# A landing buffer for the moved blocks of a feed-forward unit, and the split taken from it

## The chip, the cores and the metric

The kernel runs on one core of one Trainium2 chip. The metric is the device time of one execution in microseconds (us), the median of several runs. A core has a matrix engine (TensorE, PE in the rows; PEld are its weight loads), a vector engine (VectorE, DVE), a scalar engine (ScalarE, ACT), GpSimd (POOL) and a sync engine (SyncE, SP), whose queue issues the DMA transfers. Each engine works through its own instructions in order and waits on semaphores for the others.

## What is computed

The input x holds 8 sequences of 1024 tokens with 256 features, 8192 tokens in all. Four residual layers follow one another:

```
x = x + attention(layernorm(x))            # 2 heads, causal softmax
x = x + ffn(layernorm(x))
x = x + linear_attention(layernorm(x))     # 8 heads with decay
x = x + ffn(layernorm(x))                  # the same weights again

def ffn(x):                                # w_*: integers times 1/127
    gate = x @ wg.T;  up = x @ wu.T        # 256 -> 768
    return (silu(gate) * up) @ wd.T        # 768 -> 256
```

All is float32. For its matmuls the kernel writes an activation as a high part in the type float32r and a low part, x minus the high part, also float32r, and multiplies both.

## The kernel before

The kernel runs four phases in turn (attention_phase, feed_forward_phase as ff1, linear_attention_phase, feed_forward_phase as ff2), and x stays in on-chip memory as X all the while. Within a phase the order of every engine's work is written out by hand, one function per engine, with semaphores between them.

A feed-forward phase works in 16 **units** of 512 tokens (UN), counted u = 0 to 15. The buffers of neighbouring units alternate by a parity, par. run_units (L854) writes units 0, 13, 14 and 15 out and runs 1 to 12 in a hardware loop, two per pass. left says what comes after a unit: 2 means that two more units of the phase follow, 1 that one does, 0 that none does. In a unit the 768 hidden features are worked through in six **slots**, f = 0 to 5, of 128 features each (NF = 6). What the engines do in a slot:

- TensorE (L1044 to L1060) computes gate(f), then up(f) (L1026), four matmuls each, and then down(f-3) (L1037), the last projection of the slot three earlier (LAG = 3), eight matmuls. Slots 3, 4 and 5 of a unit are thus projected down in slots 0, 1 and 2 of the next. Gate and up have three banks each (NB_GU = 3), so gate(f) waits for the silu of slot f-3, up(f) for the h of slot f-3, and down waits for the high and the low part of its h. Ahead of its first slot a unit waits for its high and low parts (front.pe_wait, L1045).
- ScalarE (L943 to L954) takes silu(f) (L951) and then the high part of h of slot f-1 (L941).
- VectorE (L984 to L1004) takes h(f) = silu(f) * up(f) (L990), which waits for silu(f), then the low part of h of slot f-1 (L974). In slot 2 comes the residual of the unit before (L981).

Between these stands the preparation of later units, and it is what the change touches. It runs over these steps:

- In unit u VectorE prepares unit u+2: statistics of the layernorm in slots 0 and 1 (L132, L140), normalise in slot 3, behind h(3) and the low part of slot 2 (L156, four instructions), and in slot 4, behind h(4) and the low part of slot 3, one transpose of 32x32 blocks (dve_blocks, L255) from one half of ln_xn into the other. Here "blocks of unit u+2" names that result. The transpose waits for the move of unit u+1 to have landed, for that move reads the same buffer.
- GpSimd computes the reciprocal deviation for the normalise (L167, L170).
- In unit u SyncE moves the blocks of unit u+1 across partitions with 16 DMAs of 32 KB (sp_move, L266), which finishes the transpose. Their target is the low half of the pair of unit u+1, ln_xl or ff_odd_xl by parity. First it waits until the last up projection of unit u-1, which reads that pair, has ended (L893), then for the blocks of unit u+1.
- In slot 4 of unit u ScalarE waits for that landing, and takes the high part of unit u+1 from it (act_high, L271). In its order this stands ahead of silu(4).
- GpSimd then subtracts the high part from what landed, in place (pool_low, L276), which finishes the pair of unit u+1.

In unit 15 of ff1 the same steps prepare the first unit of the linear attention; in ff2 nothing follows, and SyncE also stores the finished tokens of unit u-1 behind the move (L904).

The order by hand in ScalarE's function is this:

```
for f in range(NF):
    if f == NF - 2 and upcoming:
        nfront.act_high(act, nu, npar)      # waits for the landing
    ...silu(f)...
    high_part(u, par, f - 1)
```

Of the kernel before, what the change touches and what calls it, by code (L numbers as in the profile page):

```python
# [13 lines left out]
F32 = mybir.dt.float32  # L14
# [4 lines left out]
ACT = mybir.ActivationFunctionType  # L19
AX = mybir.AxisListType  # L20

P = 128
NB, T, M = 8, 1024, 256
KT = M // P
# [3 lines left out]
UN = UT * P  # L28
# [14 lines left out]
NF = FF // P  # L43
# [16 lines left out]
class Signal:  # L60


    def __init__(self, nc, ctx, name, per):
        self.sem = ctx.enter_context(nc.semaphore(name))
        self.per = per
# [6 lines left out]
def open_signals(eng, *signals):  # L72

    for s in signals:
        eng.sem_inc(s.sem, CREDIT)


def wait_alone(eng, sem, value, passed):


    eng.wait_ge(sem, value)
    eng.sem_inc(passed, 1)
# [140 lines left out]
class Turned:  # L223
# [4 lines left out]
    def __init__(self, nc, ctx, name, ln, blocks, parts, unit=0):  # L228
        sig = lambda n, per: Signal(nc, ctx, f"{name}_{n}", per)
        self.nc, self.ln, self.blocks, self.unit = nc, ln, blocks, unit  # L230
        self.parts = [parts, parts]
        self.blocks_done = sig("blocks_done", 1)
        self.landed = sig("landed", 16 * MOVES)
        self.sp_passed = ctx.enter_context(nc.semaphore(f"{name}_sp_passed"))
        self.hi_done, self.lo_done = sig("hi_done", 1), sig("lo_done", 1)
# [19 lines left out]
        self.nc.vector.transpose(self.blocks.rearrange("p t m -> p (t m)"),  # L255
                                 self.ln.out[:, self.unit * UT:(self.unit + 1) * UT, :].rearrange("p t m -> p (t m)")).then_inc(self.blocks_done.sem, 1)

    def sp_move(self, sp, unit, par):

        wait_alone(sp, self.blocks_done.sem, self.blocks_done.at(unit, 1), self.sp_passed)  # L260
        lo = self.parts[par][1][:].bitcast(F32)
        for r in range(NQ):
            for c in range(NQ):
                src = self.blocks[r * SQ:(r + 1) * SQ, c, :].rearrange("p (n b) -> p n b", b=SQ)
                dst = lo[c * SQ:(c + 1) * SQ].rearrange("p k (t r b) -> p (k t) r b", t=UT, r=NQ)[:, :, r, :]
                sp.dma_start(dst, src).then_inc(self.landed.sem, 16)  # L266

    def act_high(self, act, unit, par):
        hi, lo = self.parts[par]
        act.wait_ge(self.landed.sem, self.landed.at(unit, 16 * MOVES))  # L270
        self.nc.scalar.activation(hi[:], lo[:].bitcast(F32), ACT.Copy).then_inc(self.hi_done.sem, 1)  # L271

    def pool_low(self, pool, unit, par):
        hi, lo = self.parts[par]
        pool.wait_ge(self.hi_done.sem, self.hi_done.at(unit, 1))  # L275
        self.nc.gpsimd.tensor_tensor(lo[:], lo[:].bitcast(F32), hi[:].bitcast(F32),  # L276
                                     ALU.subtract).then_inc(self.lo_done.sem, 1)

    def pe_wait(self, pe, unit):
# [529 lines left out]
def load_lin_weights(eng, env, io):  # L809
    stage = env["stage"]  # L810
    eng.dma_start(stage[:, 0:KT * LB_COLS].rearrange("p (k n) -> p k n", k=KT),
                  io["w_lin"].rearrange("(k p) n -> p k n", p=P)).then_inc(env["lin_loaded"], 16)
    eng.dma_start(stage[:, KT * LB_COLS:KT * LB_COLS + NP * M].rearrange("p (k m) -> p k m", k=NP),
                  io["w_o"].rearrange("(k p) m -> p k m", p=P)).then_inc(env["lin_loaded"], 16)


def feed_forward_phase(nc, env, io, name, nth, front, following):
# [5 lines left out]
    with ExitStack() as ctx:  # L823
        sb = lambda n, shape, dt=F32: ctx.enter_context(nc.sbuf_tensor(f"{name}_{n}", shape, dt))
# [9 lines left out]
        down_hi, down_lo = (w[:, parts_of_w[2]].rearrange("p (k m) -> p k m", k=NF) for w in (w_hi, w_lo))  # L834
        ln = front.ln
        front.parts[1] = sb("odd_xh", [P, KT, UN], F32R), sb("odd_xl", [P, KT, UN], F32R)
        sx = [front.pair(0), front.pair(1)]
        NB_GU = 3
        silu = sb("silu", [P, NB_GU, UN])
# [6 lines left out]
        gate_ready, up_ready = sig("gate_ready", NF), sig("up_ready", NF)  # L846
# [7 lines left out]
        def run_units(eng, unit):  # L854


            unit(0, 0, True, 2)
            with eng.Fori(0, NU // 2 - 2) as p:
                unit(p * 2 + 1, 1, False, 2)
                unit(p * 2 + 2, 0, False, 2)  # L860
            unit(NU - 3, 1, False, 2)
            unit(NU - 2, 0, False, 1)
            unit(NU - 1, 1, False, 0)

        def slot(par, f):

            return (NF * par + f) % NH

        def next_of(u, par, left):

            if left:
                return front, u + 1, 1 - par
            return (following, 0, 0) if following else None

        def after_next(u, left):

            if left == 2:
                return front, u + 2
            return (following, 0) if left and following else None

        with nc.Block() as block:

            @block.sync
            def _(sp):
                if following:
                    following.sp_open(sp)

                def unit(u, par, first, left):
                    upcoming = next_of(u, par, left)
                    if upcoming:  # L890
                        nfront, nu, npar = upcoming
                        if not first:
                            wait_alone(sp, up_ready.sem, up_ready.at(u - 1, NF), front.sp_passed)  # L893
                        nfront.sp_move(sp, nu, npar)
                    if following and first:
                        sp.wait_ge(prep_lo, NPART)
                        load_lin_weights(sp, env, io)
                    if not following and not first:
                        store(u - 1)

                def store(u):
                    wait_alone(sp, x_done.sem, x_done.at(u, 1), front.sp_passed)
                    at = bass.ds(u * UT, UT)
                    sp.dma_start(out_v[:, at, :], X[:, at, :]).then_inc(stored, 16)  # L904

                run_units(sp, unit)
                if not following:
                    store(NU - 1)
                    sp.wait_ge(stored, 16 * NU)

            @block.gpsimd
            def _(pool):
                if following:
                    following.pool_open(pool)

                def unit(u, par, first, left):
                    upcoming, after = next_of(u, par, left), after_next(u, left)
                    if after:
                        after[0].ln.pool_rstd(pool, after[1])
                    if upcoming:  # L920
                        nfront, nu, npar = upcoming
                        nfront.pool_low(pool, nu, npar)

                run_units(pool, unit)

            @block.scalar
            def _(act):
                if following:
                    following.act_open(act)
                open_signals(act, silu_done, hi_done)  # L930
                for at in parts_of_w:
                    if split_before:
                        nc.scalar.activation(w_lo[:, at], stage[:, at], ACT.Copy).then_inc(prep_lo, 1)
                    else:
                        act.wait_ge(env["ff_loaded"], 16 * NPART * nth)
                        nc.scalar.activation(w_hi[:, at], stage[:, at].bitcast(I32), ACT.Copy).then_inc(prep_hi, 1)  # L936

                def high_part(u, par, f):
                    act.wait_ge(h_done.sem, h_done.at(u, f + 1))
                    act.wait_ge(down_done.sem, down_done.at(u, f - NH + 1))  # L940
                    nc.scalar.activation(h_hi[:, slot(par, f), :], h[:, f % 2, :], ACT.Copy).then_inc(hi_done.sem, 1)  # L941

                def unit(u, par, first, left):  # L943
                    upcoming = next_of(u, par, left)
                    for f in range(NF):
                        if f == NF - 2 and upcoming:
                            nfront, nu, npar = upcoming
                            nfront.act_high(act, nu, npar)
                        act.wait_ge(gate_ready.sem, gate_ready.at(u, f + 1))
                        act.wait_ge(h_done.sem, h_done.at(u, f - NB_GU + 1))  # L950
                        nc.scalar.activation(silu[:, f % NB_GU, :], PS[:, f % NB_GU, :], ACT.Silu,  # L951
                                             scale=W_SCALE).then_inc(silu_done.sem, 1)
                        if f > 0 or not first:
                            high_part(u, par, f - 1)  # L954
                    if not left:
                        high_part(u, par, NF - 1)

                run_units(act, unit)

            @block.vector  # L960
# [678 lines left out]
```

## Time and profile before

| what | value |
|---|---|
| median of 3 runs | 1981.17 us (1980.4 to 1982.3) |
| the profiled execution, its own time | 1982.85 us |
| its span, first to last instruction | 1981.1 us |
| mean granted TensorE clock | 0.994 of full speed |
| busy share: PE, PEld, DVE, ACT, POOL | 95%, 83%, 69%, 45%, 23% |
| ff1, first matmul to last | about 565 to 846 us |
| ff2, first matmul to last | about 1698 to 1976 us |

The shares are averages over the four phases, and matmuls are pipelined, so a PE that is busy 95% of the time is not at its peak. A row of the chronological view gives the start, the duration, the engine, the line, the operation, what it writes and reads, and in brackets the idle time of the engine just before it with what ended it. SPq is the queue of SyncE; of a row with x16 the duration runs from the first issue to the end of the last.

### The profile page before, as it was taken

Reading aid. Unit: us, or ns where it says so; the run is one execution under the profiler, and the core shown is the slowest. Engines: PE = TensorE matmul, PEld = TensorE weight load, DVE = VectorE, ACT = ScalarE, POOL = GpSimd, SP = SyncE. Lnnn points to the kernel's source line nnn. Section 1 sums busy time; section 2 is a strip of 40 time slices with the busy share of each in tenths; the row PEclk is TensorE's granted clock in tenths of the full one; section 3 lists DMA queues with packets and bytes.
Section 4 is the critical chain, followed back from the end, with each engine's and each line's share of the span. In section 5 each row is a group of like instructions: output and inputs, shape, how many; then the busy total and the mean of one; then the engine's idle time right before and its main releaser. Section 6 shows DMA issues by size and latency. Waiting matters only on the chain. (4 is left out here: it accounts for less than half of the span.)

```text
span 1981.1 us, 36996 instructions
## 1 busy us (share of the span) xinstructions
PE 1891.3 (95%) x12419; PEld 1639.4 (83%) x12419; DVE 1367.3 (69%) x3222; ACT 889.7 (45%) x1708; POOL 451.7 (23%) x362
## 2 busy tenths in 40 slices
PE   6999999999989999969999999999999998899998
PEld 5888888888778888858888888888888887788887
DVE  6666566656667888756766667766666677778885
ACT  5555556655654444453333333333333332444443
POOL 2112201220312222132222222222222222221220
PEclk9999999999999999989999999999999999999999
DMA  6100000000021111110000000000000000122222
GB/s 217 58 1 0 0 0 0 0 0 0 12 75 30 30 30 30 32 53 11 12 12 12 11 11 11 11 11 11 11 11 11 11 12 12 32 64 63 53 61 58
DMA packets 230887, 53.23 MB, mean 27 GB/s; under 512 B 209952, under 2 KB 229024, under 8 KB 230432
## 3 DMA queue, kind: packets, MB, share of 16 engines
q1 hardware_dynamic: 229696, 49.54, 11.7%
q10 hardware_dynamic: 1120, 2.75, 0.4%
q8 instruction: 43, 0.70, 0.2%
q14 instruction: 28, 0.23, 0.0%
HBM read 18.69 MB, written 8.39 MB: 14 GB/s over the span
## 5 line engine op out<-in xcount | busy, mean ns | idle before, releaser
L990 DVE SCALAR_TENSOR_TENSOR ff_h<-PS,ff_silu 128x512 f32<-128x512 f32 x192 | 130.9, 682 | 121.9 <-PE PS L1026 53.2
L951 ACT ACTIVATE ff_silu<-PS 128x512 f32<-128x512 f32 x192 | 114.0, 595 | 199.7 <-PE PS L1026 199.7
L1214 POOL TENSOR_TENSOR lin_yg_lo<-stage,lin_yg_hi 128x512 fp32r<-128x512 f32 x64 | 82.0, 1281 | 504.5 <-ACT lin_yg_hi L1248 504.5
L1037 PE MATMUL PS<-ff_w_hi,ff_h_hi 128*128 128x256 f32 x768 | 191.3, 282 | 2.1 <-ACT ff_h_hi L941 1.4
L1037 PE MATMUL PS<-ff_w_hi,ff_h_lo 128*128 128x256 f32 x768 | 191.9, 283 | 0.0
L318 PE MATMUL PS<-ln_xh,lin_w_hi 128*128 128x512 f32 x384 | 153.4, 400 | 15.6 <-DVE lin_w_lo L1293 8.6
L974 DVE TENSOR_TENSOR ff_h_lo<-ff_h,ff_h_hi 128x512 fp32r<-128x512 f32 x192 | 164.2, 855 | 0.2
L1026 PE MATMUL PS<-ln_xh,ff_w_hi 128*128 128x512 f32 x384 | 152.0, 396 | 11.6 <-issue 4.5
L730 PE MATMUL PS<-probT,v_a 128*128 128x128 f32 x1152 | 154.0, 279 | 4.3 <-DVE oT_lo L589 4.3
L1324 DVE TENSOR_TENSOR lin_AD<-PS,lin_decay 128x512 f32<-128x512 f32 x128 | 82.2, 684 | 109.9 <-PE PS L1470 109.9
L1037 PEld LDWEIGHTS PS<-ff_w_hi,ff_h_hi 128*128 128x128 f32 x768 | 145.6, 190 | 13.7 <-issue 2.9
L1026 PE MATMUL PS<-ff_odd_xh,ff_w_hi 128*128 128x512 f32 x384 | 151.8, 395 | 5.2 <-issue 2.4
L730 PEld LDWEIGHTS PS<-probT,v_a 128*128 128x128 f32 x1152 | 138.9, 192 | 19.5 <-issue 12.9
L318 PE MATMUL PS<-ln_xh,lin_w_lo 128*128 128x512 f32 x384 | 151.3, 394 | 0.0
L1037 PEld LDWEIGHTS PS<-ff_w_hi,ff_h_lo 128*128 128x128 f32 x768 | 146.3, 190 | 6.0
L318 PE MATMUL PS<-ln_xl,lin_w_hi 128*128 128x512 f32 x384 | 151.0, 393 | 0.0
L1026 PE MATMUL PS<-ff_odd_xl,ff_w_hi 128*128 128x512 f32 x384 | 150.8, 393 | 0.0
L1026 PE MATMUL PS<-ln_xl,ff_w_hi 128*128 128x512 f32 x384 | 150.6, 392 | 0.0
L702 PE MATMUL PS<-qk 128*128 128x512 f32 (+3 forms) x384 | 144.7, 488 | 0.0
L594 DVE TENSOR_REDUCE neg_max<-PS 128x1 f32<-128x256 f32 (+7 forms) x128 | 96.6, 755 | 65.5 <-PE PS L705 64.3
L455 POOL TENSOR_TENSOR qk<-qk,swapped 64x512 f32<-64x512 f32 x64 | 81.9, 1280 | 256.1 <-DVE swapped L584 254.2
L271 ACT ACTIVATE ln_xh<-ln_xl 128x1024 fp32r<-128x1024 f32 x32 | 33.9, 1060 | 232.2 <-DMA ln_xl<-ln_xn 232.2
(159 smaller groups left out, 4893.1 us busy)
## 6 DMA issues: line engine op xcount, KB each, us to landing
ln_xl<-ln_xn SPq DMA_DIRECT2D x512, 32.0 KB, 2.0
X<-in_x SPq DMA_DIRECT2D x8, 1024.0 KB, 5.3
ff_odd_xl<-ln_xn SPq DMA_DIRECT2D x256, 32.0 KB, 2.0
out_x<-X SPq DMA_DIRECT2D x16, 512.0 KB, 2.9
stage<-in_w_lin SPq DMA_DIRECT2D x1, 2048.0 KB, 8.2
stage<-in_w_gate SPq DMA_DIRECT2D x2, 768.0 KB, 4.3
stage<-in_w_up SPq DMA_DIRECT2D x2, 768.0 KB, 5.8
stage<-in_w_down SPq DMA_DIRECT2D x2, 768.0 KB, 7.5
```

The costliest lines, as they stand in the source:

```text
L318: last = nc.tensor.matmul(out, w, x, start=n == 0, stop=n == len(terms) - 1)
L455: done = nc.gpsimd.tensor_tensor(qk[rows, s, h, at], qk[rows, s, h, at], swapped[rows, 2 * half + s, :], ALU.add)
L594: nc.vector.tensor_reduce(neg_max[:, n:n + 1], score_rows(n), AX.X, ALU.max, negate=True).then_inc(max_done.sem, 1)
L702: last = nc.tensor.matmul(bank[:, 0:w], qk[:, 0, h, i * P:(i + 1) * P], qk[:, 1, h, c:c + w], start=True, stop=not diag)
L730: last = nc.tensor.matmul(O, V[:, j, h * DA:(h + 1) * DA], probT[:, n % 2, j, :], start=j == 0, stop=j == i)
L951: nc.scalar.activation(silu[:, f % NB_GU, :], PS[:, f % NB_GU, :], ACT.Silu, scale=W_SCALE).then_inc(silu_done.sem, 1)
L974: nc.vector.tensor_tensor(h_lo[:, slot(par, f), :], h[:, f % 2, :], h_hi[:, slot(par, f), :].bitcast(F32), ALU.subtract).then_inc(lo_done. ...
L990: nc.vector.scalar_tensor_tensor(h[:, f % 2, :], PS[:, NB_GU + f % NB_GU, :], W_SCALE, silu[:, f % NB_GU, :], ALU.mult, ALU.mult).then_inc ...
L1026: ins = nc.tensor.matmul(PS[:, bank, :], w, x, start=n == 0, stop=n == len(parts) - 1)
L1037: ins = nc.tensor.matmul(Y[:, t // 2, (t % 2) * M:(t % 2 + 1) * M], a[:, slot(par, f), t * P:(t + 1) * P], w[:, f % NF, :], start=f == 0 a ...
L1214: nc.gpsimd.tensor_tensor(yg_lo[:], yg, yg_hi[:].bitcast(F32), ALU.subtract).then_inc(yg_lo_done.sem, 1)
L1324: nc.vector.tensor_tensor(AD[:, c % 2, r], PS[:, r, :].rearrange("p (j t) -> p j t", t=P), D[:].rearrange("p (j r) t -> p r j t", r=2)[:, ...
```

## The change

A buffer raw of the size of one half of a pair (128 x 1024 float32) is added to each feed-forward phase. The move of a unit's blocks lands in it whenever the unit belongs to the same phase (raw=bool(left)); ScalarE takes the high part from raw, and GpSimd subtracts the high part from raw and writes the low half of the pair. Three things in the order change with it. SyncE waits ahead of the move of unit u+1 for the low part of unit u (the last reader of raw), and not for the last up projection of unit u-1. ScalarE waits for that projection in SyncE's place. And ScalarE takes the high part of the coming unit in slot 3 (NF - 3), ahead of silu(3), and no longer in slot 4. The move into the linear attention's first unit keeps the old target, wait and slot.

```diff
--- before.py
+++ after.py
@@ -229,6 +229,7 @@
         sig = lambda n, per: Signal(nc, ctx, f"{name}_{n}", per)
         self.nc, self.ln, self.blocks, self.unit = nc, ln, blocks, unit
         self.parts = [parts, parts]
+        self.raw = None
         self.blocks_done = sig("blocks_done", 1)
         self.landed = sig("landed", 16 * MOVES)
         self.sp_passed = ctx.enter_context(nc.semaphore(f"{name}_sp_passed"))
@@ -255,25 +256,29 @@
         self.nc.vector.transpose(self.blocks.rearrange("p t m -> p (t m)"),
                                  self.ln.out[:, self.unit * UT:(self.unit + 1) * UT, :].rearrange("p t m -> p (t m)")).then_inc(self.blocks_done.sem, 1)
 
-    def sp_move(self, sp, unit, par):
+    def landing(self, par, raw):
+
+        return self.raw[:] if raw else self.parts[par][1][:].bitcast(F32)
+
+    def sp_move(self, sp, unit, par, raw=False):
 
         wait_alone(sp, self.blocks_done.sem, self.blocks_done.at(unit, 1), self.sp_passed)
-        lo = self.parts[par][1][:].bitcast(F32)
+        lo = self.landing(par, raw)
         for r in range(NQ):
             for c in range(NQ):
                 src = self.blocks[r * SQ:(r + 1) * SQ, c, :].rearrange("p (n b) -> p n b", b=SQ)
                 dst = lo[c * SQ:(c + 1) * SQ].rearrange("p k (t r b) -> p (k t) r b", t=UT, r=NQ)[:, :, r, :]
                 sp.dma_start(dst, src).then_inc(self.landed.sem, 16)
 
-    def act_high(self, act, unit, par):
+    def act_high(self, act, unit, par, raw=False):
         hi, lo = self.parts[par]
         act.wait_ge(self.landed.sem, self.landed.at(unit, 16 * MOVES))
-        self.nc.scalar.activation(hi[:], lo[:].bitcast(F32), ACT.Copy).then_inc(self.hi_done.sem, 1)
-
-    def pool_low(self, pool, unit, par):
+        self.nc.scalar.activation(hi[:], self.landing(par, raw), ACT.Copy).then_inc(self.hi_done.sem, 1)
+
+    def pool_low(self, pool, unit, par, raw=False):
         hi, lo = self.parts[par]
         pool.wait_ge(self.hi_done.sem, self.hi_done.at(unit, 1))
-        self.nc.gpsimd.tensor_tensor(lo[:], lo[:].bitcast(F32), hi[:].bitcast(F32),
+        self.nc.gpsimd.tensor_tensor(lo[:], self.landing(par, raw), hi[:].bitcast(F32),
                                      ALU.subtract).then_inc(self.lo_done.sem, 1)
 
     def pe_wait(self, pe, unit):
@@ -834,6 +839,7 @@
         down_hi, down_lo = (w[:, parts_of_w[2]].rearrange("p (k m) -> p k m", k=NF) for w in (w_hi, w_lo))
         ln = front.ln
         front.parts[1] = sb("odd_xh", [P, KT, UN], F32R), sb("odd_xl", [P, KT, UN], F32R)
+        front.raw = sb("raw", [P, KT, UN])
         sx = [front.pair(0), front.pair(1)]
         NB_GU = 3
         silu = sb("silu", [P, NB_GU, UN])
@@ -889,9 +895,12 @@
                     upcoming = next_of(u, par, left)
                     if upcoming:
                         nfront, nu, npar = upcoming
-                        if not first:
+                        if left:
+                            if not first:
+                                wait_alone(sp, front.lo_done.sem, front.lo_done.at(u, 1), front.sp_passed)
+                        else:
                             wait_alone(sp, up_ready.sem, up_ready.at(u - 1, NF), front.sp_passed)
-                        nfront.sp_move(sp, nu, npar)
+                        nfront.sp_move(sp, nu, npar, raw=bool(left))
                     if following and first:
                         sp.wait_ge(prep_lo, NPART)
                         load_lin_weights(sp, env, io)
@@ -919,7 +928,7 @@
                         after[0].ln.pool_rstd(pool, after[1])
                     if upcoming:
                         nfront, nu, npar = upcoming
-                        nfront.pool_low(pool, nu, npar)
+                        nfront.pool_low(pool, nu, npar, raw=bool(left))
 
                 run_units(pool, unit)
 
@@ -943,9 +952,11 @@
                 def unit(u, par, first, left):
                     upcoming = next_of(u, par, left)
                     for f in range(NF):
-                        if f == NF - 2 and upcoming:
+                        if f == (NF - 3 if left else NF - 2) and upcoming:
                             nfront, nu, npar = upcoming
-                            nfront.act_high(act, nu, npar)
+                            if left and not first:
+                                act.wait_ge(up_ready.sem, up_ready.at(u - 1, NF))
+                            nfront.act_high(act, nu, npar, raw=bool(left))
                         act.wait_ge(gate_ready.sem, gate_ready.at(u, f + 1))
                         act.wait_ge(h_done.sem, h_done.at(u, f - NB_GU + 1))
                         nc.scalar.activation(silu[:, f % NB_GU, :], PS[:, f % NB_GU, :], ACT.Silu,
```

## Rows read from the trace of the kernel before

**Rows 1.** The page, busy time and share of the span of each engine:
```profile
PE 1891.3 (95%) x12419; PEld 1639.4 (83%) x12419; DVE 1367.3 (69%) x3222; ACT 889.7 (45%) x1708; POOL 451.7 (23%) x362
```

**Rows 2.** Waits of SyncE's queue, 600 to 800 us: total, times, longest:
```profile
SPq L82 <- PE PS L1026: 41.1, 11, 4.0
SPq L82 <- DVE ln_xn L255: 31.9, 12, 4.3
```

**Rows 3.** Chronological view of SyncE's queue, one move of ff1:
```profile
721.25 10.46 SPq L266 DMA_DIRECT2D ln_xl<-ln_xn  x16
```

**Rows 4.** The same view, ScalarE, slot 4 of three units in a row:
```profile
698.78 1.06 ACT L271 ACTIVATE ln_xh<-ln_xl 128x1024 fp32r<-128x1024 f32 x1 [2.71 <-DMA ln_xl<-ln_xn]
...
715.90 1.06 ACT L271 ACTIVATE ff_odd_xh<-ff_odd_xl 128x1024 fp32r<-128x1024 f32 x1 [2.61 <-DMA ff_odd_xl<-ln_xn]
716.87 0.58 ACT L951 ACTIVATE ff_silu<-PS 128x512 f32<-128x512 f32 x1
...
733.09 1.06 ACT L271 ACTIVATE ln_xh<-ln_xl 128x1024 fp32r<-128x1024 f32 x1 [2.66 <-DMA ln_xl<-ln_xn]
```

**Rows 5.** The same view, VectorE, slots 3 and 4 of that unit:
```profile
713.70 0.68 DVE L974 TENSOR_TENSOR ff_h_lo<-ff_h,ff_h_hi 128x512 fp32r<-128x512 f32 x1
714.30 1.38 DVE L156 TENSOR_SCALAR ln_xn<-X,ln_mean_var,ln_rstd 128x256 f32 x4
717.54 0.69 DVE L990 SCALAR_TENSOR_TENSOR ff_h<-PS,ff_silu 128x512 f32<-128x512 f32 x1 [1.85 <-issue]
718.14 1.86 DVE L974 TENSOR_TENSOR ff_h_lo<-ff_h,ff_h_hi 128x512 fp32r<-128x512 f32 x1
719.92 1.23 DVE L255 STREAM_TRANSPOSE ln_xn<-ln_xn 128x1024 f32<-128x1024 f32 x1
```

**Rows 6.** The same view, GpSimd, the low part of the coming unit:
```profile
717.04 2.41 POOL L276 TENSOR_TENSOR ff_odd_xl<-ff_odd_xl,ff_odd_xh 128x1024 fp32r<-128x1024 f32 x1 [6.18 <-ACT ff_odd_xh L271]
```

**Rows 7.** The same view, TensorE, from one unit into the next:
```profile
701.97 0.28 PE L1037 MATMUL PS<-ff_w_hi,ff_h_hi 128*128 128x256 f32 x1
702.09 0.28 PE L1037 MATMUL PS<-ff_w_hi,ff_h_lo 128*128 128x256 f32 x1
702.57 0.49 PE L1026 MATMUL PS<-ln_xh,ff_w_hi 128*128 128x512 f32 x1 [0.20 <-POOL ln_xl L276]
```

**Rows 8.** The page, groups: a GpSimd subtraction out of one buffer into another:
```profile
L1214 POOL TENSOR_TENSOR lin_yg_lo<-stage,lin_yg_hi 128x512 fp32r<-128x512 f32 x64 | 82.0, 1281 | 504.5 <-ACT lin_yg_hi L1248 504.5
```

**Rows 9.** The first unit of ff1, VectorE and ScalarE:
```profile
575.29 1.06 ACT L271 ACTIVATE ff_odd_xh<-ff_odd_xl 128x1024 fp32r<-128x1024 f32 x1 [0.71 <-DMA ff_odd_xl<-ln_xn]
...
575.85 3.47 DVE L156 TENSOR_SCALAR ln_xn<-X,ln_mean_var,ln_rstd 128x256 f32<-128x256 f32 x4
579.24 0.68 DVE L990 SCALAR_TENSOR_TENSOR ff_h<-PS,ff_silu 128x512 f32<-128x512 f32 x1
...
580.44 1.23 DVE L255 STREAM_TRANSPOSE ln_xn<-ln_xn 128x1024 f32<-128x1024 f32 x1
```

**Rows 10.** The first unit of ff2, ScalarE and VectorE:
```profile
1707.99 1.06 ACT L271 ACTIVATE ff_odd_xh<-ff_odd_xl 128x1024 fp32r<-128x1024 f32 x1 [0.44 <-DMA ff_odd_xl<-ln_xn]
...
1713.45 1.23 DVE L255 STREAM_TRANSPOSE ln_xn<-ln_xn 128x1024 f32<-128x1024 f32 x1
```

**Rows 11.** High parts taken last in ff1 and in ff2:
```profile
837.73 1.06 ACT L271 ACTIVATE ln_xh<-ln_xl 128x1024 fp32r<-128x1024 f32 x1 [2.75 <-DMA ln_xl<-ln_xn]
...
1952.83 1.06 ACT L271 ACTIVATE ff_odd_xh<-ff_odd_xl 128x1024 fp32r<-128x1024 f32 x1 [3.65 <-DMA ff_odd_xl<-ln_xn]
```

**Rows 12.** Two idle times of TensorE, late in linear attention and into ff2:
```profile
1680.73 1.24 PE L1499 MATMUL PS<-lin_v,lin_ks 128*128 128x130 f32 x4 [3.15 <-DVE lin_ks L1319]
...
1698.05 0.47 PE L1026 MATMUL PS<-ln_xh,ff_w_hi 128*128 128x512 f32 x1 [2.64 <-ACT ff_w_hi L936]
```

**Rows 13.** Stretches around them: length, busy times by engine, granted clock, DMA:
```profile
1676.00:1682.00 6.00, 2.85 (x21) 2.66 (x19) 5.31 (x11) 0.63 (x1) 1.36 (x1) 0.79 0.00 0
1682.00:1688.00 6.00, 6.00 (x36) 5.97 (x35) 3.90 (x13) 0.13 (x1) 0.00 (x0) 0.64 0.01 3
...
1697.00:1702.00 5.00, 3.85 (x16) 2.92 (x17) 4.17 (x3) 4.97 (x5) 0.00 (x0) 1.00 0.29 46
```

## The prediction

> **What bounds the kernel now.** The page's first part shows TensorE busy for 95% of the span [rows 1], which invites the reading that only matmul time counts. It is an average, and a matmul row is longer than the pitch at which matmuls follow one another, so I read one feed-forward unit in order of time, engine by engine, looking for the chain that closes from unit to unit.
>
> The natural start is the waits of SyncE's queue, since the change replaces one of them. Over 200 us, nearly 12 units, it waited 41.1 us for TensorE's up projection and 31.9 us for the transposed blocks [rows 2]. A reader may take the first number for the price of the wait that is removed. But the two waits stand one behind the other ahead of each move, and the blocks come last: in one unit the transpose starts at 719.92 and takes 1.23, so it ends at 721.15 [rows 5], and the first DMA is issued at 721.25 [rows 3]. The wait for TensorE had by then been over for some time. What starts a move is the transpose.
>
> From there the chain runs on. All times are starts unless said otherwise:
> - first DMA 721.25, high part 733.09 [rows 3, 4]: 11.84 us, of which 10.46 is issuing the 16 DMAs one after another. ScalarE had idled 2.66 us for this landing.
> - high part 715.90, silu(4) behind it 716.87 [rows 4], h(4) 717.54, low part of slot 3 718.14, transpose 719.92 [rows 5]: 4.02 us from high part to transpose. The low part took 1.86 us where the same operation took 0.68 at 713.70 [rows 5]; GpSimd's own subtraction ran from 717.04 to 719.45 [rows 6], and VectorE's low part ended 0.55 us after it. I read this as VectorE held back until GpSimd was done.
> - transpose 719.92 to first DMA 721.25: 1.33 us.
>
> The sum is 4.02 + 1.33 + 11.84 = 17.19 us from one high part to the next, and rows 4 show just that from 715.90 to 733.09, and 17.16 on average over two units from 698.78. TensorE is not in this chain. It fills its unit and then waits 0.36 us: the down matmuls start 0.12 apart, the last at 702.09, so the next could start at 702.21, and it came at 702.57 [rows 7]. So TensorE alone needs 17.12 (698.78 to 715.90) - 0.36, about 16.8 us per unit. **The feed-forward phases are bound by the chain landing, high part, silu, h, low part, transpose, move, landing, with TensorE close below it.**
>
> One more thing matters in the same rows: VectorE does its normalise (714.30, 1.38 us) while it would otherwise idle; even so it idled 1.85 us before h(4) [rows 5]. Today that work costs the chain nothing.
>
> **The change part by part.** *SyncE's wait.* Removed: the wait for the up projection, worth nothing, since the transpose ends later. Added: a wait for the low part of unit u. It ends 719.45 in rows 6, ahead of the transpose's end at 721.15, so it costs nothing either: SyncE gets no earlier start from the new buffer. In ff2 the store stands behind the move in the same queue, and waits for a residual of slot 2; nothing there is new.
>
> *ScalarE's wait for the up projection.* In steady state it has long been met when the landing comes, for ScalarE idles 2.6 us there [rows 4]. Cost nothing; cover is that idle time.
>
> *The buffer.* The high part and the subtraction read as many elements as before, from another address. I take 1.06 and 2.41 us as they are [rows 4, 6]. No row shows this subtraction from one buffer into another. The nearest one of half the size does, 1.28 us [rows 8]; twice that, 2.56, counts its fixed part twice and is the upper bound, 0.15 us more in each link, some 4 us in all. Below, the bound is no change, since the elements and types are the same; rows 6 are the same operation, so I take them.
>
> *The high part in slot 3.* This is the part that costs. It can't be taken before its blocks land, and they land about 12 us behind the transpose in slot 4 of the unit before. ScalarE works in order, so silu(3) is now held by the landing, where it was silu(4). Behind silu(3) VectorE's order is h(3), low part of slot 2, normalise, h(4), low part of slot 3, transpose. So from the high part on:
> - silu(3) takes the place of silu(4), h(3) that of h(4), the low part of slot 2 that of slot 3, still held by GpSimd: the next VectorE instruction starts 4.02 us after the high part, as the transpose did.
> - it is the normalise, whose cover is gone: 1.38 us, and the next start comes 0.08 before a row's end (575.85 + 3.47 against 579.24 in rows 9), so 1.30.
> - h(4) and the low part of slot 3: 0.60 each from start to start (717.54 to 718.14, and 713.70 to 714.30 for a low part that isn't held, in rows 5). GpSimd is idle by then.
> - transpose at 4.02 + 1.30 + 0.60 + 0.60 = 6.52 us.
>
> The link becomes 6.52 + 1.33 + 11.84 = 19.69 us, **2.50 us more in every unit**. TensorE needs 16.8, so it no longer sets anything, and idles 2.9 us per unit, in slot 5 ahead of down(2), which waits for the held low part.
>
> Could the phase settle elsewhere, with the landing ahead of slot 3? A unit paced by TensorE alone has slots of 2.8 us. up(4) would end 4 x 2.8 + 1.9 = 13.1 us into the unit; h(4), a low part and the transpose follow at 0.6 + 0.6 + 1.2, the move adds 11.8 and the hand-over 0.1: landed 27.4 us after the unit's start, 10.6 into the next. gate(3) is ready at 3 x 2.8 + 0.9 = 9.3. So even from an undisturbed start silu(3) is late, and the chain above takes over.
>
> *How many links.* ff1 prepares units 1 to 15 and then the linear attention's first unit, which makes 15 links between 16 high parts (575.29 to 837.73 [rows 9, 11]); 14 of them gain 2.50 = 35.0. In the first, the normalise is caught by GpSimd already (3.47 us) and the transpose came at 575.29 + 5.15; it moves to + 6.52, a cost of 1.4. The last high part stays in slot 4, and the end of ff1 hangs on it as before. ff1: 36.4 us. ff2 has 14 links; 13 x 2.50 = 32.5, and the first costs 1707.99 + 6.52 - 1713.45 = 1.1 [rows 10]. Behind its last high part (1952.83 [rows 11]) the last unit starts once down(2) is through, 4.1 + 0.9 = 5.0 us later, where it started 702.57 - 698.78 = 3.8 after the high part in steady state [rows 4, 7], so 1.2 more. ff2: 34.8 us. Attention and linear attention keep their instructions.
>
> **Sum:** 36.4 + 34.8 = 71.2 us on the profiled execution's 1982.85 us: 2054.1. That execution stands 1.7 us above the median of the runs, so for the median I say 1981.2 + 71.2 = **2052.4 us**, 3.6% slower.
>
> *The clock.* TensorE's granted clock is at the full level of 2.4 GHz in the feed-forward phases. One idle time of 3.15 us at 1680.73 [rows 12] was followed by a fall: 0.79 and 0.64 granted in two stretches of 6 us, between its two levels, 1.2 and 2.4 GHz [rows 13]. One of 2.64 us at 1698.05 was not: 1.00 [rows 12, 13]. The new idle time, 2.9 us, lies between. If it fell each time as it did there, the loss would be 6 x 0.21 + 6 x 0.36 = 3.4 us of matmul work, against 2.9 us of slack: 0.5 us per unit over some 29 units, 14 us more. I leave it out of the sum, since the slack takes nearly all and a unit without slack has no idle time to cause the next fall.
>
> The Trainium skill, page "TensorE: Matmul & The Clock Gate", section "Why this matters for your kernels", speaks against this change here: it warns that idle stretches between bursts of matmuls bring the lower clock back. By it the sum would be the clock case's 2066; rows 12 and 13 agree for one idle time and not for the other.
>
> **The rivals.**
> - *The buffer lets the moves start early (faster).* For it: 41.1 us of waiting for TensorE [rows 2]. If that wait were the last, the chain would fall below TensorE's pace and each phase would run at 16.8 per unit: ff1 837.73 - 575.29 - 15 x 16.76 = 11.0, ff2 1952.83 - 1707.99 - 14 x 16.76 = 10.2 [rows 9 to 11], so about 1960. It decides once the landing comes before gate(3) is ready. Against it: the move starts 0.1 us behind the transpose. 4%.
> - *The place of the high part makes no difference (the same).* For it: silu results have three buffers and the down projections lag by three slots, so late silus need not stop TensorE. Against it: it is VectorE's transpose, not TensorE, that is delayed. About 1981. 3%.
> - *VectorE gets ahead of GpSimd.* If the low part of slot 2 weren't held (0.68 instead of 1.86), a link would gain 1.2 less: 2.50 - 1.18 = 1.3, or 71 - 28 x 1.18 = 38: 2019. Against it: GpSimd starts 1.1 us behind the high part, 1.1 us ahead of the low part, as now. 3%.
> - *The clock falls as well:* 2066, or somewhat above if the lower level lasts longer. 9%.
> - The chain as worked out, 2052: 81%.
>
> **How the numbers follow.** 0.2% (4 us) is about what measurement can tell from no change. Faster 0.04, same 0.03, slower 0.93. Within the main case the link's cost may lie between 2.2 and 2.8 us (hand-overs, and a stretch of DMA issues that takes 11.3 in place of 10.4), 9 us either way. With the clock case the range is 2041 to 2067; it leaves out the low rivals.
>
> **What would show it.** Right: in slot 3 ScalarE idles for the DMA before the high part, 19.7 us from one high part to the next; the normalise directly behind a low part of 1.8 us; the transpose 6.5 us behind the high part; the first DMA 0.1 us behind the transpose's end; TensorE idle some 2.9 us per unit at L1037, waiting for the low part of h; the linear attention as long as before. Wrong: a move issued before the transpose ends (impossible by its data), high parts 17 us apart or closer, or a granted clock well below 1 in ff1.

## The result, and the profile after

| | before | after |
|---|---|---|
| median | 1981.74 us (4 runs) | 2054.07 us (4 runs, 2053.64 to 2057.85) |
| span of the profiled execution | 1981.1 us | 2051.8 us |
| mean granted clock | 0.994 | 0.981 |

The change makes the kernel slower: ratio 1.037, 95% interval 1.0352 to 1.0388. Forecast were 2052.4 us and a range of 2041 to 2067.

The page of the changed kernel, its busy times and one group of its fifth part (TensorE's down projection), against [rows 1]:

```profile
PE 1913.5 (93%) x12419; PEld 1653.6 (81%) x12419; DVE 1361.4 (66%) x3222; ACT 887.6 (43%) x1708; POOL 458.2 (22%) x362
...
L1048 PE MATMUL PS<-ff_w_hi,ff_h_hi 128*128 128x256 f32 x768 | 201.1, 293 | 60.7 <-DVE ff_h_lo L985 59.0
```

The instructions of the computing engines are the same in number, and none got more than a little busier (TensorE's 22 us more go with its lower clock, on which more below). What is new is 59 us in which TensorE waits at the down projection for a low part of h. (Lines have moved: act_high is L276, pool_low L281, transpose L256, h L1001, its low part L985, down L1048, the move's DMA L271.)

The chronological view of the changed kernel, ScalarE, which answers to [rows 4]:

```profile
716.20 1.06 ACT L276 ACTIVATE ln_xh<-ff_raw 128x1024 fp32r<-128x1024 f32 x1 [5.03 <-DMA ff_raw<-ln_xn]
717.16 0.58 ACT L962 ACTIVATE ff_silu<-PS 128x512 f32<-128x512 f32 x1
...
735.81 1.06 ACT L276 ACTIVATE ff_odd_xh<-ff_raw 128x1024 fp32r<-128x1024 f32 x1 [6.51 <-DMA ff_raw<-ln_xn]
```

VectorE between the two, which answers to [rows 5], and GpSimd, to [rows 6]:

```profile
717.83 0.69 DVE L1001 SCALAR_TENSOR_TENSOR ff_h<-PS,ff_silu 128x512 f32<-128x512 f32 x1 [4.44 <-ACT ff_silu L962]
718.44 1.84 DVE L985 TENSOR_TENSOR ff_h_lo<-ff_h,ff_h_hi 128x512 fp32r<-128x512 f32 x1
720.21 1.37 DVE L156 TENSOR_SCALAR ln_xn<-X,ln_mean_var,ln_rstd 128x256 f32 x4
721.50 0.69 DVE L1001 SCALAR_TENSOR_TENSOR ff_h<-PS,ff_silu 128x512 f32<-128x512 f32 x1
722.10 0.68 DVE L985 TENSOR_TENSOR ff_h_lo<-ff_h,ff_h_hi 128x512 fp32r<-128x512 f32 x1
722.70 1.24 DVE L256 STREAM_TRANSPOSE ln_xn<-ln_xn 128x1024 f32<-128x1024 f32 x1
...
717.34 2.40 POOL L281 TENSOR_TENSOR ln_xl<-ff_raw,ln_xh 128x1024 fp32r<-128x1024 f32 x1 [6.03 <-ACT ln_xh L276]
```

And the queue of SyncE, to [rows 3], in a window from 715 to 728 us, which cuts the row off after 7 of the 16 DMAs:

```profile
724.03 4.51 SPq L271 DMA_DIRECT2D ff_raw<-ln_xn  x7
```

Read them in the order of the chain. The landing releases the high part at 716.20. Behind it come silu(3), h(3), the held low part of slot 2, the normalise, h(4), the low part of slot 3 and, 6.50 us after the high part, the transpose. The first DMA is issued 1.33 later, and the next high part is taken at 735.81: 19.61 us in all, where it was 17.2. Before, VectorE did the normalise and then idled 1.85 us for silu(4); now it idles 4.44 us for silu(3), and all that stands in slot 3 comes behind.

### The profile page after: what moved, and what is told of

It is laid out like the page before. It is cut to its first block and busy times, and to the rows that moved or that the text cites. A ratio compares the mean times of both kernels' runs of the same rounds, so it can differ in the third digit from the quotient of the medians.

```text
span 2051.8 us, 37000 instructions
## 1 busy us (share of the span) xinstructions
PE 1913.5 (93%) x12419; PEld 1653.6 (81%) x12419; DVE 1361.4 (66%) x3222; ACT 887.6 (43%) x1708; POOL 458.2 (22%) x362
## 5 line engine op out<-in xcount | busy, mean ns | idle before, releaser
L1001 DVE SCALAR_TENSOR_TENSOR ff_h<-PS,ff_silu 128x512 f32<-128x512 f32 x192 | 130.3, 679 | 196.8 <-ACT ff_silu L962 118.4
L1048 PE MATMUL PS<-ff_w_hi,ff_h_hi 128*128 128x256 f32 x768 | 201.1, 293 | 60.7 <-DVE ff_h_lo L985 59.0
L1048 PEld LDWEIGHTS PS<-ff_w_hi,ff_h_hi 128*128 128x128 f32 x768 | 151.3, 197 | 83.7 <-issue 73.2
L1048 PE MATMUL PS<-ff_w_hi,ff_h_lo 128*128 128x256 f32 x768 | 198.2, 289 | 0.0
L323 PE MATMUL PS<-ln_xh,lin_w_hi 128*128 128x512 f32 x384 | 152.5, 397 | 16.7 <-DVE lin_w_lo L1304 16.3
L985 DVE TENSOR_TENSOR ff_h_lo<-ff_h,ff_h_hi 128x512 fp32r<-128x512 f32 x192 | 165.8, 863 | 0.2
L950 ACT ACTIVATE ff_h_hi<-ff_h 128x512 fp32r<-128x512 f32 x192 | 120.3, 627 | 97.7 <-DVE ff_h L1001 97.5
L1048 PEld LDWEIGHTS PS<-ff_w_hi,ff_h_lo 128*128 128x128 f32 x768 | 151.9, 198 | 5.2
L1037 PE MATMUL PS<-ff_odd_xl,ff_w_hi 128*128 128x512 f32 x384 | 156.1, 406 | 0.0
```

The costliest lines, as they stand in the source:

```text
L323: last = nc.tensor.matmul(out, w, x, start=n == 0, stop=n == len(terms) - 1)
L985: nc.vector.tensor_tensor(h_lo[:, slot(par, f), :], h[:, f % 2, :], h_hi[:, slot(par, f), :].bitcast(F32), ALU.subtract).then_inc(lo_done. ...
L1001: nc.vector.scalar_tensor_tensor(h[:, f % 2, :], PS[:, NB_GU + f % NB_GU, :], W_SCALE, silu[:, f % NB_GU, :], ALU.mult, ALU.mult).then_inc ...
L1037: ins = nc.tensor.matmul(PS[:, bank, :], w, x, start=n == 0, stop=n == len(parts) - 1)
L1048: ins = nc.tensor.matmul(Y[:, t // 2, (t % 2) * M:(t % 2 + 1) * M], a[:, slot(par, f), t * P:(t + 1) * P], w[:, f % NF, :], start=f == 0 a ...
```

## The experiments

Six kernels ask what the cost consists of, four what is to be had by the same reading. Those told as a single run have no interval. "Link" is the time from one high part to the next in the middle of ff1.

| label | what it is | us | link |
|---|---|---|---|
| before | | 1981 | 17.2 |
| changed kernel | | 2054 | 19.6 |
| e1_raw_slot4 | buffer and waits, high part in slot 4 | 1982.1 | 17.2 |
| e2_before_slot3 | no buffer, high part in slot 3 | 2053.9 | 19.6 |
| e3_norm_first | normalise ahead of h(3) | 2021.6 | 18.6 |
| e7_turn_slot4_head | transpose at the head of slot 4 | 2026.0 | 18.7 |
| e8_half_low | half of GpSimd's subtraction | 2022.1 | 18.5 |
| e4_slot2 | high part in slot 2 | 2191.0 | 23.9 to 25.1 |
| e5_before_turn_first | before, transpose ahead of h(4) | 1964.2 | 16.8 |
| e6_after_turn_first | changed, both at the head of slot 3 | 1977.1 | 17.2 |
| e9_norm_slot2 | as e6, normalise in slot 2 | 2095.6 | 20.2 to 22.9 |
| e10_turn_first_slot4 | as e6, high part in slot 4 | 1966.8 | 16.8 |

**The two halves of the change apart (e1, e2).** e1, against the changed kernel:

```diff
-                        if f == (NF - 3 if left else NF - 2) and upcoming:
+                        if f == NF - 2 and upcoming:
```

> The changed kernel with the high part of the coming unit back in slot 4; the buffer raw and both new waits stay. By the chain (the cost is VectorE's normalise, h(4) and low part put between landing and transpose) everything comes back: 17.2 us from one high part to the next, 1982 us, give or take 3. If the cost comes from the buffer or from SyncE's wait for the low part, it stays near 2054. If it were the late silus holding TensorE, slot 4 would give back only the part of one slot, with a figure between the two.

e2 makes the same edit the other way round in the kernel before, and nothing else.

> The kernel before with the high part in slot 3 and nothing else: no buffer, old waits. By the chain it costs all that the change costs: 19.6 us per unit, 2053 us, give or take 4. If the buffer or its waits cost something, it comes out lower by that; if they are the whole cost, 1982.

e1: 1982.11 us, ratio to before 0.9999, interval 0.9987 to 1.0011. e2: 2053.93, ratio 1.0357 (1.0337 to 1.0377). e2 in the chronological view, ScalarE and VectorE:

```profile
714.05 1.06 ACT L271 ACTIVATE ln_xh<-ln_xl 128x1024 fp32r<-128x1024 f32 x1 [5.02 <-DMA ln_xl<-ln_xn]
...
733.65 1.06 ACT L271 ACTIVATE ff_odd_xh<-ff_odd_xl 128x1024 fp32r<-128x1024 f32 x1 [6.52 <-DMA ff_odd_xl<-ln_xn]
...
720.54 1.23 DVE L255 STREAM_TRANSPOSE ln_xn<-ln_xn 128x1024 f32<-128x1024 f32 x1
```

The transpose comes 6.49 us behind the high part and the link is 19.60, without any buffer. So the whole cost is the slot of the high part, and the buffer with its two waits is worth nothing that e1 can tell, which is some 2 us either way. That is so although SyncE's row of waits grew. The waits of its queue over the whole changed kernel:

```profile
SPq L82 <- POOL ln_xl L281: 63.3, 14, 5.0
SPq L82 <- POOL ff_odd_xl L281: 57.4, 14, 4.8
```

These 120.7 us stand where 95.0 us of waiting for TensorE stood. Neither is a price, for behind them in the same queue stands the wait for the blocks, which ends last: in the rows of the changed kernel GpSimd's low part was done at 719.74 and the transpose at 723.94, and the first DMA came at 724.03.

**The terms of the link, one at a time (e3, e7, e8, e4).** e3 and e7 move an operation of VectorE out of the chain:

```diff
 e3: for f in range(NF):
+    if after and f == 3: after[0].ln.dve_normalise(dve, after[1])
     dve.wait_ge(up_ready.sem, up_ready.at(u, f + 1))
...
 e7: for f in range(NF):
+    if after and f == 4: after[0].dve_blocks(dve, after[1], (front, u + 1))
     dve.wait_ge(up_ready.sem, up_ready.at(u, f + 1))
```

(Each call is shown on one line with its condition, and is gone from its old place.)

> The changed kernel with VectorE's normalise ahead of h(3) in slot 3, so ahead of the held wait, high part still in slot 3. By the chain a link loses the normalise's 1.30 us: transpose 5.2 us behind the high part, 18.3 us per unit, 2054 - 28 x 1.30 = 2018 us. If late silus or TensorE's clock set the pace, the place of the normalise is nothing to them and it stays near 2054.

> The changed kernel with the transpose at the head of slot 4, ahead of h(4) and the low part of slot 3, normalise left in slot 3. By the chain a link loses these two, 2 x 0.60: transpose 5.3 us behind the high part, 18.4 us per unit, 2054 - 28 x 1.20 = 2020 us. The rival that late silus hold TensorE directly gives 2054.

e3: 2021.61 us in a single run; e7: 2026.00 in a single run. Both came down as the chain has it, by 32.5 and 28.1 us where 36 and 34 were expected. The rows of e3 (ScalarE, VectorE):

```profile
725.74 1.06 ACT L276 ACTIVATE ff_odd_xh<-ff_raw 128x1024 fp32r<-128x1024 f32 x1 [5.42 <-DMA ff_raw<-ln_xn]
...
727.98 1.83 DVE L985 TENSOR_TENSOR ff_h_lo<-ff_h,ff_h_hi 128x512 fp32r<-128x512 f32 x1
729.95 0.69 DVE L1003 SCALAR_TENSOR_TENSOR ff_h<-PS,ff_silu 128x512 f32<-128x512 f32 x1
731.16 1.24 DVE L256 STREAM_TRANSPOSE ln_xn<-ln_xn 128x1024 f32<-128x1024 f32 x1
```

The transpose is 5.42 us behind the high part and not 5.20: h(4) starts 0.14 after the low part's end, where rows usually overlap by 0.08. That hand-over of 0.2 us is what I had not priced, and no run shows its cause. e7 has one like it at its transpose, 5.54 us behind the high part where 5.32 were expected. Over 28 links it makes some 6 us, about what e3 and e7 fell short by (4 and 6).

e8 tests my reading of the slow low part, that GpSimd holds VectorE. It leaves out the subtraction for half the features, whose low parts keep old values:

```diff
-  ...tensor_tensor(lo[:], self.landing(par, raw), hi[:].bitcast(F32), ALU.subtract)
+  ...tensor_tensor(lo[:, part, :], self.landing(par, raw)[:, part, :], hi[:, part, :].bitcast(F32), ALU.subtract)
   # part: half the features, but all of them in the first unit
```

> The changed kernel with GpSimd's subtraction cut to one of the two halves of the features in all but the first unit of a phase (the low parts of the other half keep old values, so this part of the computation is left out). If GpSimd's 2.4 us hold VectorE's low part, it ends 2.4 us behind the high part and holds VectorE no longer: the low part of slot 2 takes 0.7 instead of 1.8 us, the link loses 1.1 us, 18.5 us per unit, some 2054 - 27 x 1.1 = 2024 us. If VectorE's slow low part has another cause (ScalarE's own reads, the DMA), it stays at 1.8 us and 2054.

2022.13 us in a single run (2024 expected). GpSimd and VectorE in e8; the high part was taken at 726.77:

```profile
727.91 1.28 POOL L281 TENSOR_TENSOR ff_odd_xl<-ff_raw,ff_odd_xh 128x512 fp32r<-128x512 f32 x1 [5.67 <-ACT ff_odd_xh L276]
...
729.02 0.72 DVE L985 TENSOR_TENSOR ff_h_lo<-ff_h,ff_h_hi 128x512 fp32r<-128x512 f32 x1
...
732.16 1.23 DVE L256 STREAM_TRANSPOSE ln_xn<-ln_xn 128x1024 f32<-128x1024 f32 x1
```

With GpSimd done at 729.19, the low part takes 0.72 in place of 1.84, and the transpose comes 5.39 us behind the high part. The hold is real, and worth 1.1 us per link.

e4 puts the high part one more slot ahead (NF - 4).

> The changed kernel with the high part another slot earlier, in slot 2. By the chain VectorE's residual (1.14 us from start to start), h(3) and the low part of slot 2 (0.60 each) come into the link: 2.3 us more, 22.0 us per unit, 2054 + 28 x 2.34 = 2120 us. If ScalarE's wait merely ends with the same landing and only that counts, the place of the high part makes no further difference: 2054.

2191 us, a single run: the direction is the chain's, the size is not (2120). ScalarE, VectorE and TensorE in e4:

```profile
721.46 1.06 ACT L276 ACTIVATE ff_odd_xh<-ff_raw 128x1024 fp32r<-128x1024 f32 x1 [5.27 <-DMA ff_raw<-ln_xn]
...
725.41 1.21 DVE L992 SCALAR_TENSOR_TENSOR X<-PS,X 128x1024 f32 x1
...
726.68 0.58 PE L1048 MATMUL PS<-ff_w_hi,ff_h_hi 128*128 128x256 f32 x1 [5.23 <-DVE X L992]
...
732.05 0.69 DVE L1001 SCALAR_TENSOR_TENSOR ff_h<-PS,ff_silu 128x512 f32<-128x512 f32 x1 [2.94 <-PE PS L1037]
...
733.25 1.24 DVE L256 STREAM_TRANSPOSE ln_xn<-ln_xn 128x1024 f32<-128x1024 f32 x1
...
746.43 1.06 ACT L276 ACTIVATE ln_xh<-ff_raw 128x1024 fp32r<-128x1024 f32 x1 [5.73 <-DMA ff_raw<-ln_xn]
```

The residual of slot 2 now stands behind the landing, and down(0) in slot 3 waits for it: TensorE idles 5.23 us. Its first work afterwards, down(0) and gate and up of slot 4, is what h(4) waits for, so TensorE has come into the chain; and it runs at the lower clock. The stretches of 6 us of e4 (length, busy times, granted clock, DMA):

```profile
718.00:724.00 6.00, 3.44 (x19) 2.65 (x18) 0.91 (x2) 2.54 (x5) 2.43 (x2) 1.00 0.17 27
724.00:730.00 6.00, 3.32 (x12) 3.04 (x13) 5.11 (x8) 0.52 (x2) 0.94 (x1) 0.57 0.00 0
730.00:736.00 6.00, 6.00 (x32) 5.19 (x31) 3.61 (x5) 2.23 (x4) 0.00 (x0) 0.86 0.02 2
```

From TensorE's first matmul at 726.68 to h(4) at 732.05 are 5.37 us. The same stretch took 3.08 us in a unit of e9 (below) in which the clock stayed at the full level. Over 26 units of e4 it took 4.35 to 5.53 us, 4.8 on average, so the lower clock cost about 1.7 us per unit, some 48 over 28 units. The rest is mostly TensorE's own path: even at the full clock the transpose would stand 5.22 + 3.1 + 1.2 = 9.5 us behind the high part, where I had expected 6.50 + 2.34 = 8.8, and 0.7 us per unit makes some 19. By this estimate the two make 67 of the 71 us between 2120 and 2191; no run takes them apart.

**What the reading is good for (e5, e6, e9, e10).** If the transpose waits only for the landing, the link is 1.33 + 11.84 = 13.2 us, below TensorE's 16.8. e5 makes e7's move in the kernel before. e6 puts normalise and transpose at the head of slot 3 of the changed kernel, e9 the normalise into slot 2 ahead of the residual, e10 is e6 with the high part in slot 4.

```diff
 e6, e10: for f in range(NF):
+    if after and f == 3: after[0].ln.dve_normalise(dve, after[1])
+    if after and f == 3: after[0].dve_blocks(dve, after[1], (front, u + 1))
     dve.wait_ge(up_ready.sem, up_ready.at(u, f + 1))
```

> The kernel before with the transpose of slot 4 put ahead of h(4), so that it waits for the landing alone and not for high part, silu, h and low part. By the chain the link falls from 17.2 to 1.33 + 11.84 = 13.2 us, below TensorE's 16.8, which then sets the pace: about 1960 us, no idle time of TensorE between units. If TensorE's 0.36 us per unit has another cause, or VectorE holding h(4) for the transpose costs as much, it stays at 1981.

> The changed kernel (buffer, waits, high part in slot 3) with VectorE's normalise and transpose at the head of slot 3, ahead of h(3). By the chain the landing then comes 3.6 us before the next transpose, ahead of gate(3), and TensorE's 16.8 us set the pace here too: about 1960 us, so the slot of the high part costs nothing once the transpose no longer stands behind it. If slot 3 as such costs, because ScalarE is taken from the silus, it stays well above 1981.

e5: 1964.21 us, ratio to before 0.9916 (0.9903 to 0.9929). e6: 1977.06, ratio 0.9982 (0.9974 to 0.9991), a miss by 17. First e5, VectorE and its 200 us from 600 on:

```profile
711.12 3.47 DVE L156 TENSOR_SCALAR ln_xn<-X,ln_mean_var,ln_rstd 128x256 f32 x4
...
727.88 1.38 DVE L156 TENSOR_SCALAR ln_xn<-X,ln_mean_var,ln_rstd 128x256 f32 x4
729.42 1.25 DVE L255 STREAM_TRANSPOSE ln_xn<-ln_xn 128x1024 f32<-128x1024 f32 x1 [0.15 <-DVE ln_xn L156]
...
600.00:800.00 200.00, 200.00 (x1148) 175.22 (x1148) 168.41 (x312) 93.48 (x156) 45.31 (x36) 1.00 0.20 31
```

TensorE is busy in all 200 us, and 14 links from 576.52 to 811.23 average 16.77 us. In every second unit GpSimd's subtraction holds the normalise (3.47 us at 711.12), and the links alternate between 17.2 and 16.3, but TensorE doesn't wait for it. Then e6, ScalarE, GpSimd, VectorE:

```profile
713.82 1.06 ACT L276 ACTIVATE ff_odd_xh<-ff_raw 128x1024 fp32r<-128x1024 f32 x1 [1.68 <-DMA ff_raw<-ln_xn]
...
714.96 2.39 POOL L281 TENSOR_TENSOR ff_odd_xl<-ff_raw,ff_odd_xh 128x1024 fp32r<-128x1024 f32 x1 [2.69 <-ACT ff_odd_xh L276]
...
714.28 3.54 DVE L156 TENSOR_SCALAR ln_xn<-X,ln_mean_var,ln_rstd 128x256 f32 x4
717.97 1.25 DVE L256 STREAM_TRANSPOSE ln_xn<-ln_xn 128x1024 f32<-128x1024 f32 x1
```

Here the normalise is the one that GpSimd holds, 3.54 us for 1.38, as in the first units of before [rows 9]. It stands ahead of the transpose, so a chain closes again: landing, high part, subtraction, held normalise, transpose, 17.2 us.

> As the kernel before this one (changed kernel, high part in slot 3, transpose at the head of slot 3), but the normalise in slot 2, ahead of the residual, so that it isn't caught by GpSimd's subtraction right ahead of the transpose. If that held normalise (3.5 us in place of 1.4) is what kept the kernel before this one at 17.2 us per unit, the link falls to about 13.2 us, TensorE's 16.8 sets the pace, and it takes 1964 us as the old kernel with the transpose first does. If instead ScalarE's high part in slot 3 costs by itself, it stays near 1977.

> As the kernel that took 1977 us (changed kernel, normalise and transpose at the head of slot 3), with only the high part put back from slot 3 to slot 4. If that kernel's 17.2 us per unit come from the chain landing, high part, GpSimd's subtraction, normalise held by it, transpose, then the later high part lets the normalise run free (1.4 us), the landing comes ahead of slot 4, and TensorE's 16.8 set the pace: 1964 us. If its cost lies in the transpose standing ahead of h(3), the slot of the high part makes no difference: 1977.

e9: 2095.6 us, ratio 1.0574 (1.0549 to 1.0598), a plain miss. The landing no longer holds ScalarE (its high part has no idle time before it), but this normalise is held too, and now stands ahead of the residual. VectorE and TensorE in e9:

```profile
718.02 3.52 DVE L156 TENSOR_SCALAR ln_xn<-X,ln_mean_var,ln_rstd 128x256 f32 x4
721.46 1.21 DVE L992 SCALAR_TENSOR_TENSOR X<-PS,X 128x1024 f32 x1
...
722.73 0.50 PE L1048 MATMUL PS<-ff_w_hi,ff_h_hi 128*128 128x256 f32 x1 [3.16 <-DVE X L992]
```

TensorE idles 3.16 us for the residual in each unit, and 16.8 + 3.2 = 20.0 us is nearly the link of 20.2 that comes where the clock stays up. In most units it then works on at a lower clock, 0.91 granted on average from 600 to 840 us, and the link is 21.7 to 22.9. Two stretches from TensorE's first matmul to the next h that waits for it show the price:

```profile
679.71 0.38 PE L1048 MATMUL PS<-ff_w_hi,ff_h_hi 128*128 128x256 f32 x1 [3.16 <-DVE X L992]
...
679.71:682.79 3.08, 3.08 (x18) 2.75 (x19) 2.26 (x3) 0.91 (x2) 0.00 (x0) 1.00 0.07 11
722.73:727.38 4.65, 4.65 (x18) 4.08 (x19) 2.26 (x3) 0.94 (x2) 0.00 (x0) 0.63 0.17 27
```

The second takes 1.57 us more for the same work, and its link of 21.73 is 1.56 longer than the first's, 20.17: here, with TensorE in the chain, a fall of the clock is paid in full. The order broke one chain and closed another. e9 thus doesn't test what e6 lost, since its normalise was held again; e10 does. e10: 1966.84 us, ratio 0.9927 (0.9913 to 0.9940), where 1964 were expected; its normalise and transpose take 1.37 and 1.25 us, and links are 16.8:

```profile
728.73 1.05 ACT L276 ACTIVATE ln_xh<-ff_raw 128x1024 fp32r<-128x1024 f32 x1
...
728.17 1.37 DVE L156 TENSOR_SCALAR ln_xn<-X,ln_mean_var,ln_rstd 128x256 f32 x4
729.69 1.25 DVE L256 STREAM_TRANSPOSE ln_xn<-ln_xn 128x1024 f32<-128x1024 f32 x1 [0.15 <-DVE ln_xn L156]
```

So with the transpose out of the way the slot of the high part is still worth 10 us (e6 against e10), by what GpSimd holds. The lowest time here is e5's, the old kernel with one call moved: 1964 us, 16 us (0.8%) faster than before and 90 faster than the changed one. Its interval overlaps that of e10, so the two aren't told apart.

## Why the prediction was right

- *What starts a move is the transpose, and SyncE's removed and added waits cost nothing.* Right, and shown by e1: 0.9999, interval 0.9987 to 1.0011. GpSimd's subtraction out of raw took 2.35 to 2.41 us in ff1 where rows 6 have 2.41, so the upper bound for the buffer wasn't needed.
- *The high part in slot 3 puts normalise, h(4) and a low part into the chain.* Right; e2 shows that it is the whole cost, e3 and e7 that its terms can be taken out.
- *6.52 us from high part to transpose, a link of 19.69.* Measured 6.50 (716.20 to 722.70) and 19.61.
- *The hold of VectorE by GpSimd.* Read off one overlap; e8 shows it.
- *The sum.* The 15 links of ff1 took 874.50 - 577.16 = 297.3 us against 262.4, so 34.9 more (36.4 forecast). The 14 of ff2 took 2021.47 - 1744.03 = 277.4 against 244.8, 32.6 more (33.6 forecast); behind them 30.3 us against 28.2, 2.1 more (1.2 forecast). The rest, 1.9 us by which attention took longer and 0.7 by which linear attention took less, is in instructions that nobody touched: the first high part came between 575.3 and 577.3 in the kernels of this study. The three differences in ff1, ff2 and the end come to 69.6, where 71.2 were forecast.
- *The clock.* Left out of the sum, rightly. TensorE's idle times in the changed kernel, and stretches of 5 us:

```profile
700.75 0.36 PE L1048 MATMUL PS<-ff_w_hi,ff_h_hi 128*128 128x256 f32 x1 [2.58 <-DVE ff_h_lo L985]
...
720.43 0.36 PE L1048 MATMUL PS<-ff_w_hi,ff_h_hi 128*128 128x256 f32 x1 [1.12 <-DVE ff_h_lo L985]
...
702.00:707.00 5.00, 5.00 (x20) 4.18 (x19) 4.97 (x8) 1.86 (x3) 0.00 (x0) 0.66 0.09 14
...
722.00:727.00 5.00, 5.00 (x31) 4.42 (x30) 4.97 (x9) 2.87 (x5) 0.00 (x0) 1.00 0.12 20
```

Behind 2.58 us of idling the clock fell (0.66 granted, 5 x 0.34 = 1.7 us of work lost), which used up most of the next unit's slack, so the next idle time was 1.12 us and nothing fell. From 642 to 819 us the units alternate like this, and the links next to each other are 19.61 and 19.63 us all the same. Two units in a row fell ahead of that, behind 3.29 us of idling (601.70) and behind 1.97 (622.23). The granted clock of ff1 was 0.96 on average (565 to 885 us). The prediction had named a clock well below 1 in ff1 as a sign of being wrong; the clock did fall in 8 units of ff1, and the period did not move, so that sign was badly chosen. The fall cost 1.7 us of work and not the 3.4 of the clock case, so it stayed below the slack. The Trainium skill's warning that idle stretches between bursts of matmuls bring the lower clock back (page "TensorE: Matmul & The Clock Gate", section "Why this matters for your kernels") holds here for the clock in those 8 units and not for the time; in e4 and e9, where TensorE is in the chain, it holds for the time as well.

What the prediction got slightly wrong is TensorE's new idle time: 2.9 us in each unit were forecast, 59.0 us in 29 waits came, 2.0 on average. The difference is about the work lost to the lower clock: 4% of ff1's 320 us, over 15 units, is 0.85 us per unit.

## What to carry to other kernels

A wait that is long in the table of waits has a price only if nothing ends later in the same queue; look for the event that does, and follow it around until the chain closes, for that chain's length is the period. An instruction that waits for a late event should stand as late in its engine's order as its readers allow, and an instruction that starts a long transfer as early as its data allow: here moving the waiter one slot ahead cost 72 us (e2), and moving the starter ahead of two instructions gained 16 (e5). When an order is changed, ask of each neighbour what it now stands behind, and what runs beside it on GpSimd.

## What was unexpected about the hardware

- The length of an idle time of TensorE doesn't by itself say whether the clock falls. 2.58 us at 700.75 in the changed kernel was followed by 0.66 granted over 5 us. The 2.64 us ahead of the first matmul of ff2 were followed by 1.00 in the kernel before (1698.05 [rows 12, 13]), and in e2 by 0.79 and 0.64 in two stretches of 3 us (1732.35). In e9 3.16 us were followed by a fall in most units, and by 1.00 at 679.71 and 788.95. What decides it no run here shows.
- A clock that falls after idle time can cost nothing or everything: 1.7 us of work in every second unit hidden in the changed kernel, 1.6 us paid in full in the unit of e9 shown above.
- GpSimd's subtraction held VectorE's normalise (1.4 to 3.5 us) as it holds its two-input subtraction, but no transpose or h: wherever e5, e6, e9 and e10 show one beside it, h took 0.65 to 0.70 us and the transpose 1.23 to 1.25.
